# Third joint pass of a five-stage token model, without the preparation of a group past the last

## The reference, cut to what matters

```python
h = token_stage(x, itok)                  # 16 sequences of 128 tokens, width 192
h = h + prefix_attention(layernorm(h))    # 12 heads of 16
h = h + routed_layer(layernorm(h))        # 19 of 128 tokens attend, all go through a 768-wide FFN
h = h + low_rank_attention(layernorm(h))  # 12 heads, softmax
h = h + top2_of_8_experts(layernorm(h))   # 192 -> 768 -> 192

def token_stage(sents, wids, ...):
    e = word_emb[sents] + pos_emb[:S][None, :, :] + type_emb[0][None, None, :]
    b = (e - mean(e)) * rsqrt(var(e) + 1e-12) * ln_gamma + ln_beta
    a = sigmoid(einsum('bsh,oh->bso', b, gate_w) + gate_b)
    g = einsum('bsd,hd->bsh', wvec[wids], g2b_w) + g2b_b
    return (1.0 - a) * b + a * g
```

## Time and profile before

| | |
|---|---|
| median of 3 runs | 883.57 us (882.9 to 883.79) |
| the profiled execution | 883.04 us, of which the span is 881.2 us |
| mean granted clock of TensorE | 0.931 of full speed |
| busy, share of the span | PE 82%, DVE 59%, ACT 34%, POOL 28% |
| instructions | PE 5500, DVE 1752, ACT 688, POOL 300 |

### The profile page before, as it was taken

The page is one execution under the profiler, slowest core; times in us unless marked ns, Lnnn a source line. Parts: engine busy times, 40 slices in busy tenths (PEclk is TensorE's granted clock), DMA queues, the critical chain, the costliest instruction groups (busy, mean ns, idle before and its releaser), DMA issues.

```text
span 881.2 us, 15579 instructions
## 1 busy us (share of the span) xinstructions
PE 726.0 (82%) x5500; PEld 549.1 (62%) x5501; DVE 519.7 (59%) x1752; ACT 301.4 (34%) x688; POOL 242.8 (28%) x300
## 2 busy tenths in 40 slices
PE   0888777989678998868898977959767999999993
PEld 0546465566457565646666655745456988998892
DVE  7558757874678884668877466791344553333330
ACT  0033232624333263434244334313233423333330
POOL 5332200460013245001444200231001453333332
PEclk9999989999988999998899996798897999999997
DMA  7950000000000000000121000029001233222220
GB/s 248 412 244 2 0 1 1 19 8 1 1 1 32 24 19 7 1 2 1 37 37 8 1 2 2 5 94 361 27 1 28 42 73 46 36 37 38 36 35 8
DMA packets 29894, 43.63 MB, mean 50 GB/s; under 512 B 5355, under 2 KB 24597, under 8 KB 29830
## 3 DMA queue, kind: packets, MB, share of 16 engines
q1 hardware_dynamic: 19250, 30.87, 10.2%
q0 software_dynamic: 8752, 9.07, 6.4%
q10 hardware_dynamic: 1828, 2.84, 0.9%
HBM read 21.36 MB, written 22.09 MB: 49 GB/s over the span
## 4 chain that ended last, share of the span: by engine, by line
PE 59%; DVE 21%; issue 6%; ACT 5%; POOL 4%; DMA 3%; ACTq 1%; SPq 1%; DVEq 0%; POOLq 0%
PE qc L1829 26%; PE qa L1829 25%; PE qc L1832 4%; PE qa L1832 4%; DVE mx L1424 2%; DMA out<-qk_T 2%; DVE st L1036 1%; POOL arena_w L435 1%; DMA mu_row<-in_mu 1%; ACT big L791 1%; DVE qk_T L1430 1%; DVE arena_b L1376 1%; ACTq L627 1%; DVE arena_e L1250 1%; DVE xb L1053 1%
## 5 line engine op out<-in xcount | busy, mean ns | idle before, releaser
L1829 PE MATMUL qc<-arena_w,big 128*128 x468 | 82.8, 327 | 1.4 <-DVE qk_T L1808 1.4
L1829 PEld LDWEIGHTS qc<-arena_w,big 128*128 128x128 f32 x468 | 75.1, 190 | 2.1 <-issue 2.0
L1829 PE MATMUL qa<-arena_b 128*128 128x128 f32 (+2 forms) x688 | 73.6, 289 | 3.0 <-DVE att L1440 2.1
L1829 PEld LDWEIGHTS qa<-arena_b 128*128 128x128 f32 (+2 forms) x688 | 64.9, 192 | 11.7 <-issue 2.8
L1829 PE MATMUL qa<-arena_e,nT 128*128 128x192 f32 (+2 forms) x256 | 70.0, 430 | 1.1 <-DVE ga L1320 0.7
L1002 ACT ACTIVATE big<-qa,arena_b 128x128 f32<-128x128 f32 x156 | 43.0, 374 | 75.8 <-PE qc L1829 68.7
L597 POOL DMA_INDIRECT out<-qk_T x39 | 61.0, 1565 | 20.5 <-issue 10.5
L1797 DVE COPY arena_b<-qc 128x256 f32<-128x256 f32 x39 | 16.6, 426 | 84.1 <-PE qc L1832 84.1
L1829 PEld LDWEIGHTS qa<-arena_e,nT 128*128 128x128 f32 x256 | 47.4, 200 | 23.0 <-issue 12.9
L471 POOL TENSOR_TENSOR rs_a<-rs_a,minus_half 128x8 f32<-128x8 f32 x4 | 6.6, 1644 | 175.6 <-DVE rs_a L1287 175.6
L475 POOL TENSOR_TENSOR rs_b<-rs_b,minus_half 128x4 f32<-128x4 f32 x12 | 12.5, 1041 | 152.2 <-DVE rs_b L1049 152.2
(11 more groups left out here) (366 smaller groups left out, 1576.5 us busy)
## 6 DMA issues: line engine op xcount, KB each, us to landing
slots<-xk SPq DMA_DIRECT2D x1, 13192.0 KB, 43.1
arena_e<-in_w SPq DMA_DIRECT2D x8, 579.0 KB, 7.7
arena_w<-in_w SPq DMA_DIRECT2D x8, 576.0 KB, 9.4
qk_T<-slots SPq DMA_DIRECT2D x39, 97.0 KB, 1.9
out<-hb SPq DMA_DIRECT2D x16, 96.0 KB
arena_e<-in_w_l SPq DMA_DIRECT2D x1, 804.0 KB
arena_e<-in_W ACTq DMA_DIRECT2D x1, 768.0 KB
out<-qk_T POOLq DMA_INDIRECT x39, 3.5
```

Of the source, the lines that this page charges most:

```text
L1829: return nc.tensor.matmul(o, l, r, start=start, stop=stop)
```

## The change

In `joint(3, 2)` the preparation of a fourth group is left out on all engines: each of its steps is called only `if ta + 1 < NG`. The waits for its semaphores (`g_diff` in `mix` and in the wide `logits`) go with it, and the final waits of SP and POOL count NG groups in place of NG + 1. The zero columns of `idx_all`, and the instruction that filled them, are gone; with them the tiles allocated after `idx_all` lie 32 bytes lower on each partition. Turns 1 and 2 are unchanged. The cut diff, one edit of each kind:

```diff
-        idx_all = sb("idx_all", [128, 2, B + G], I32)
+        idx_all = sb("idx_all", [128, 2, B], I32)
...
-            sp.wait_ge(s["gathered"], (NG + 1) * PER["gathered"])
-            sp.wait_ge(s["gathered_v"], (NG + 1) * PER["gathered_v"])
+            sp.wait_ge(s["gathered"], NG * PER["gathered"])
+            sp.wait_ge(s["gathered_v"], NG * PER["gathered_v"])
             sp.wait_ge(s["hin"], NG * PER["hin"])
-            sp.wait_ge(s["ln1"], (NG + 1) * PER["ln1"])
+            sp.wait_ge(s["ln1"], NG * PER["ln1"])
...
-            pool.memset(idx_all[:, :, B:B + G], 0).then_inc(fills, 1)
...
                 residual(tb, 3)
-                next_vectors(ta + 1)
+                if ta + 1 < NG:
+                    next_vectors(ta + 1)
                 root_back(tb, "ln5")
-                token_root(ta + 1)
+                if ta + 1 < NG:
+                    token_root(ta + 1)
                 scale_k(ta, 1)
                 scale_k(ta, 2)
...
                 mask(ta, 2, 0)
-                token_dot(ta + 1)
+                if ta + 1 < NG:
+                    token_dot(ta + 1)
                 mask(ta, 2, 1)
...
                 mixed(ta, 1)
-                token_diff(ta + 1)
+                if ta + 1 < NG:
+                    token_diff(ta + 1)
                 route_norm(ta, 0)
                 route_norm(ta, 1)
-                token_mix(ta + 1)
+                if ta + 1 < NG:
+                    token_mix(ta + 1)
                 mix_in(ta, 0)
-                ln1_stats(ta + 1)
+                if ta + 1 < NG:
+                    ln1_stats(ta + 1)
                 mix_in(ta, 1)
...
                 w(ta, "mixT", 4 * hf + 4)
-                w(ta + 1, "g_diff", 4)
+                if ta + 1 < NG:
+                    w(ta + 1, "g_diff", 4)
...
                 route_logits(ta, 0)
-                words_T(ta + 1)
+                if ta + 1 < NG:
+                    words_T(ta + 1)
                 route_logits(ta, 1)
                 gates_T(tb)
-                word_vectors(ta + 1)
+                if ta + 1 < NG:
+                    word_vectors(ta + 1)
```

More of the change, by code:

```diff
@@ L443, in _ @@
             pool.tensor_copy(idx_cur[:, :, :], idx_all[:, :, 0:G]).then_inc(fills, 1)
-            pool.wait_ge(fills, 3)
+            pool.wait_ge(fills, 2)
             gather_rows(0)
@@ L547, in joint @@
                 residual(tb, 0)
-                next_words(ta + 1)
+                if ta + 1 < NG:
+                    next_words(ta + 1)
                 residual(tb, 1)
@@ L552, in joint @@
                 residual(tb, 3)
-                next_vectors(ta + 1)
+                if ta + 1 < NG:
+                    next_vectors(ta + 1)
                 root_back(tb, "ln5")
-                token_root(ta + 1)
+                if ta + 1 < NG:
+                    token_root(ta + 1)
                 scale_k(ta, 1)
                 scale_k(ta, 2)
-                scale_token(ta + 1, 0)
-                scale_token(ta + 1, 1)
+                if ta + 1 < NG:
+                    scale_token(ta + 1, 0)
+                    scale_token(ta + 1, 1)
                 scale_k(ta, 3)
@@ L565, in joint @@
                 scatter(tb, 1)
-                ln1_root(ta + 1)
+                if ta + 1 < NG:
+                    ln1_root(ta + 1)
                 scatter_done(tb)
@@ L610, in _ @@
             back(NG - 1)
-            pool.wait_ge(s["gathered"], PER["gathered"] * (NG + 1))
-            pool.wait_ge(s["gathered_v"], PER["gathered_v"] * (NG + 1))
+            pool.wait_ge(s["gathered"], PER["gathered"] * NG)
+            pool.wait_ge(s["gathered_v"], PER["gathered_v"] * NG)
             pool.wait_ge(scattered, 16 * 2 * B)
@@ L942, in joint @@
                 pselT_evac(ta)
-                word_vectors(ta + 1)
+                if ta + 1 < NG:
+                    word_vectors(ta + 1)
                 route_exp(ta, 0)
-                token_gate(ta + 1)
+                if ta + 1 < NG:
+                    token_gate(ta + 1)
                 route_exp(ta, 1)
@@ L1158, in _ @@
             dve.wait_ge(setup_v, n)
-            dve.wait_ge(fills, 4)
+            dve.wait_ge(fills, 3)
             ln1_apply(0)
@@ L1597, in joint @@
                 score_max(ta)
-                token_stats(ta + 1)
+                if ta + 1 < NG:
+                    token_stats(ta + 1)
                 coefficients(ta)
@@ L1608, in joint @@
                 scale_q(ta, 2)
-                token_apply(ta + 1)
+                if ta + 1 < NG:
+                    token_apply(ta + 1)
                 spread(ta, 0)
@@ L1670, in joint @@
                 contexts(ta, 1)
-                ln1_apply(ta + 1)
+                if ta + 1 < NG:
+                    ln1_apply(ta + 1)
                 rows_out(tb, 0)
@@ L2083, in logits @@
                     w(tb, "hin", 2 * G)
-                    w(tb + 1, "g_diff", G)
+                    if tb + 1 < NG:
+                        w(tb + 1, "g_diff", G)
                 else:
```

## The result

The changed kernel takes 885.19 us (884.65 to 887.52) beside 882.79 us (879.46 to 884.87) for the kernel before: ratio 1.0032, 95% interval [1.0019, 1.0046]. Every execution of it had a mean clock of 0.906 to 0.916. It is slower, by 2.4 us, where 4.65 us less were forecast. The profiled execution took 885.05 us with a span of 883.2.

What follows compares the result with a forecast made beforehand. The chain of waits (PE 59%, DVE 21%) was taken to bound the kernel. Terms 0.95 - 0.7 + 4.4 = 4.65 us gave 878.4 us profiled, 878.9 us forecast; its own range 877.1 to 880.7, the wider one 876.6 to 881.4.

Steps and rivals of the forecast that it cites:

- Place 3: Third turn's end: mixing products and contexts start earlier without the removed steps; a gain of 4.4 us, bounds 3.2 to 5.9.
- The back turn and the expert tiles last as long as before: Sign for the profile after: these stretches behind the third turn keep their durations.
- the clock takes it back, and more: Rival: the back turn spends 13 us more at TensorE's lower level, giving 885.4 us; chance 0.04.
- Place 1: Between two masks on DVE in the third turn: removing `token_dot` ends PE's wait; gain 0.95 us, bounds 0 to 1.19.
- Place 2: Fifth norm: without `token_root`, POOL's large products start earlier and hold DVE's instructions; loss 0.7 us, bounds 0 to 1.35.
- The residual additions moved under `ln4_apply`: Third turn: two additions move up by about 5.3 us once gathers go; costed at nothing, bounds 0 to 0.3 us loss.
- less than 4 us a refutation: Sign at the third turn's end: contexts must start at least 4 us earlier relative to the first half's maxima.
- the mask's wait: Sign in the third turn: PE's wait for the second mask, near 513 us, is gone.
- the four `xb`: Sign at the fifth norm on DVE: they take about 2.9 us instead of 2.2, the first over 1 us.
- From the turn's projections to the first weight DMA: Sign for the third turn's length: 142.8 us instead of 147.43.
- The turn's clock: Sign: a turn's granted clock outside 0.90 to 0.95 would mean that the clock decided.
- Hidden steps: Most removed steps stand in other waits and gain nothing; expert weights leave earlier, keeping 73 us of slack before their reader.

Runs made afterwards that it cites:

- e6: The changed kernel with unread PE products in PE's waits at the third turn's end and in the back turn, holding the clock there: 875.45 us, ratio 0.991.
- e9: The changed kernel with PE's 12 removed instructions (word vectors) and ACT's copy between them put back: 879.14 us, ratio 0.9951.
- e2: The kernel before with only the fourth preparation's earlier steps (gathers to `token_dot`) left out, its end kept: 892.18 us, ratio 1.0027.
- e15: The changed kernel with PE's 12 instructions, their ACT copy and a small POOL root before the large products put back: 878.93 us, ratio 0.9935.
- e14: The kernel before with four unread 384-column PE products between the back turn's value rows and logits: 886.88 us, ratio 1.0038.
- e5: The changed kernel timed once more, unaltered, beside the kernel before: 885.61 us, ratio 1.0025.
- e1: The kernel before with only the end of the fourth preparation (word vectors to first norm) left out, earlier steps kept: 892.82 us, ratio 1.0033.
- e10: The changed kernel with DVE's, POOL's and ACT's steps of the end put back, PE's 12 instructions left out: 886.39 us, ratio 1.0021.
- e8: The changed kernel with a small unread root put back on POOL between the fifth norm's root and the large products: 886.93 us.
- e13: The changed kernel with four unread PE products (three of 384 columns, one of 96) before the back turn's attention logits: 886.13 us, ratio 1.0022.
- e4: The kernel before with 30 unread 96-column PE products in PE's waits of the back turn's attention: 887.5 us, ratio 0.9969.
- e3: The changed kernel with 30 unread 96-column PE products in PE's waits of the back turn's attention: 886.58 us, ratio 0.9959.
- e11: The changed kernel with ten unread 512-column PE products at the third turn's end alone, none in the back turn: 883.52 us, ratio 0.9994.
- e7: The kernel before with unread PE products in PE's waits at the third turn's end and in the back turn: 879.21 us, ratio 0.9959.

## Why the prediction was wrong

**The step that failed** is that the clock of the end and of the back turn was taken to stay as it was. It stands in the prediction at three places. Place 3 carries the 4.87 us from the mixing products' start to the first context product over unchanged; in the changed kernel they took 578.95 - 571.10 = 7.85 us, at the lower level, and 4.87 again in e6, where the clock was held. "The back turn and the expert tiles last as long as before" put the attention at 45.96 us; it took 53.46. And "the clock takes it back, and more" got 0.04, with the argument that "what is removed on PE is short (12 instructions)". Putting these 12 back (e9), with ACT's copy between them, turns the change into a gain of 4.55 us, 883.69 to 879.14, in all five executions; without them it loses 2.4. I had costed PE's removed 0.85 us of transposes as a gain of 0.85. That they could matter was in the table by slices of the kernel before, which I had not drawn: at 568 to 571 us PE stood at the lower level, fully busy, and about to rise, with the word vectors' transposes in just that stretch.

The rival itself named the place (the back turn) and a price, 885.4 us, that fits the 885.19 measured. The fit is in part luck: it counted 13 us more at the lower level, at half a us each. By the mean clocks of the two profiles it was about 30 us more (2 x (1 - 0.914) x 883.2 = 152 us against 2 x (1 - 0.931) x 881.2 = 122, an estimate), at some 0.2 us each, since PE also waits in that time.

**What the clock was, in each profiled execution** (us and mean granted clock; kernels with fills left out). Each row is one execution:

| kernel | PE's 12 | end | attention |
|---|---|---|---|
| before | yes | 30.82, 0.83 | 45.96, 0.87 |
| e2 | yes | 30.61, 0.83 | 45.79, 0.87 |
| e9 | yes | 27.73, 0.81 | 46.60, 0.85 |
| e15 | yes | 27.39, 0.81 | 45.83, 0.89 |
| e14, start moved | yes | 30.84, 0.83 | 48.82, 0.81 |
| after | no | 29.85, 0.67 | 53.46, 0.63 |
| e5 | no | 29.84, 0.67 | 53.47, 0.63 |
| e1 | no | 30.59, 0.72 | 51.34, 0.67 |
| e10 | no | 31.63, 0.72 | 51.40, 0.67 |
| e8 | no | 28.54, 0.80 | 51.29, 0.67 |
| e13, start moved | no | 29.82, 0.67 | 48.77, 0.85 |

With the 12 instructions the end had 0.81 or more and the attention 0.81 or more; without them the end had 0.80 or less and the attention 0.63 or 0.67, but for e13. The stretches without fills of the other kernels fit: the end of e4 (with the 12) had 0.83, the end of e3 and the attention of e11 (without) 0.60 and 0.63.

**Size of the loss, by the profiled spans** (883.2 against 881.2): attention +7.5 us, all clock (e3, e4, e6, e7: 44.0 to 44.5 in both kernels once held). End -1.0 where -3.62 is its worth at equal clock (e6, e7), so the clock took about 2.6 there. FFN -0.4, experts -1.5, third turn's first part -1.6 (122.26 us in e5 again). The last -1.1, up to the third turn's first projection (442.66 for 443.76), lies in turns that the change does not touch; e5, the same kernel, has 443.98 there, so it is chance.

**Place 1: right in mechanism, size not read alone.** The wait of 1.03 us is gone and no other took its place. But PE's transposes behind it come 71.07 us after the turn's start, against 69.79. 0.78 of that is place 2; and the lower level stood from about 485.1 to 488.5 us here, where the kernel before had none up to 500 us. The two places together, forecast at 0.25 us, can't be read from e6 and e7: in the profiles the third turn's first part is 1.10 us shorter with the change (123.87 for 124.97, both at 0.93), the experts 1.0 longer, and the clock of neither was held throughout.

**Place 2: right** (forecast 0.7 us, measured 0.74), shown by e8: a root of 1.06 us on POOL in front of the large products brings the 2.19 us back. The Trainium skill (Advanced Engine Details and Errata, VectorE Performance Modes, Mode Summary) says there only that such instructions block each other, and the trace agrees (2.93 us against 2.19); the size came from rows of the kernel before.
The residual additions moved under `ln4_apply`, costed at nothing (0 to 0.3), cost DVE 0.66 us: 2.55 after, 1.89 before. PE lost less: its next long products start 14.87 us after the turn's start (457.53 us) in place of 14.74 (458.50), 0.13 us later and within the bounds.

```profile
450.79 2.55 DVE L1059 TENSOR_SCALAR xb<-x,mv,rs_b 128x192 f32<-128x192 f32 x4
```
```profile
451.88 1.89 DVE L1053 TENSOR_SCALAR xb<-x,mv,rs_b 128x192 f32<-128x192 f32 x4
```

**Place 3: the chain right at a held clock, 4.4 us forecast, 3.73 there; in the changed kernel itself it failed.** The chain is the forecast one (mixing behind four `mixed`, DVE waiting for context products, the last `selected_in` earlier). But from the maxima of the first half to the contexts the changed kernel takes 12.97 us against 13.90, 0.93 less, where the prediction called less than 4 us a refutation. With the clock held it is 10.74 (e6) against 14.47 (e7), 3.73 less, still short of 4. The missing 0.67 us: `mixed` began only 0.35 us sooner behind the first logits, not 0.85 (5.49 for 5.84 us), and mixing 1.28 us behind it, not 1.1. (By its own terms the lower bound of 3.2 us is 4.4 - 1.1 = 3.3.) In e9, which keeps the 0.85 us of word transposes, 3.05 us of the remaining 3.5 are there; DVE waited 1.35 us for the contexts where about 1 was expected.

**The prediction's other signs.** The counts of instructions, the mask's wait and the four `xb` came as said. From the turn's projections to the first weight DMA it took 144.82 us, not 142.8. The turn's clock, 0.91, stayed within 0.90 to 0.95, by which the clock would not have decided: that sign looked at the whole turn, and the loss lies in its last 23 us and in the back turn.

**Hidden steps: right.** The first weight DMA leaves at 587.48 us and its first reader runs at 667.48, 80 us later.

```profile
667.48 0.77 DVE L1816 COPY arena_b<-arena_e 128x1158 f32 x1 [0.47 <-issue]
```

**What stays open.** Why the attention, which begins some 50 us after PE's missing products, keeps its clock with them and loses it without them in the table above. Holding the end's clock alone didn't do it in the one profile (e11), moving the start did (e13) but does not foretell it (e14). Nor are the 12 instructions the only way to the faster execution: of ten executions without them, e10 had two at 880.77 and 881.82 us with clocks of 0.929 and 0.927, e13 three at 881.39 to 882.42 with 0.925 to 0.927, whose attention no profile shows. So the 12 make the good pattern steady here; that they alone decide is not shown. A link through the time at which the attention's waits fall against the clock's changes fits e13 and not e14; it is argued, not shown.

## What to carry to other kernels

Before you take work off TensorE, even a product that nobody reads, look at the granted clock in short slices around it: where the level is low and about to rise, the work may be paying for the products behind it, and a removal near 1 us can cost several. Then compare the old and the new kernel once with the clock held by filler products in TensorE's waits: that separates what a change is worth (about 3.8 us here) from what is measured with the clock left free (a loss of 2.4). And time several executions of each: one profile shows one pattern of the clock. The fastest kernel here is the change with such fillers and the small root, 871.42 us.

## What the runs showed of the hardware

- **Products that nobody reads can save time.** In the kernel before, fills in the waits gave 0.9959 [0.9946, 0.9973], 3.7 us; in the changed kernel they gave 0.991 [0.9897, 0.9924], where without them it has 1.0025 [1.0012, 1.0038] on the same chip. With the change, the fills and the small root together the time is 12 us under the kernel before (0.9873 [0.9852, 0.9894]).
- **A busy PE can stay at the lower level.** In the changed kernel's attention PE was busy 42.35 of 53.46 us (79%), yet stood at 1.2 GHz from 642.1 us on for 37 us; in the kernel before it was busy 71% of the time at a mean of 0.87. The same products take longer at the lower level, so the busy share rises with it: here the kernel with the higher share is the one that stays low. The Trainium skill (TensorE: Matmul & The Clock Gate, HAM oscillation — how this bites in real kernels) looks for the cause of a falling clock in long idle gaps of TensorE. The traces do not bear that out as the difference here. Both kernels have a wait of 1.94 us behind their first attention logits, and both fall near its end (at 646.5 us before, at 642.1 after). The kernel before is back at 650.0 and up until 667, with waits of up to 1.17 us in between; the changed kernel stays low, with none above 0.80 until 673 us.
- **One kernel, one chip, 1.5% apart.** On the first chip the kernel before ran from 884.65 us at 0.931 to 897.86 at 0.911, on the others from 879.46 to 887.6. One code also showed two clocks in one stretch: the end took 29.85 us at 0.67 in the changed kernel and 34.29 at 0.60 in e3, which has the same instructions up to there. A difference of a few us needs the clock beside each time.
